# A gate term taken from tables in DRAM by one 48-row matmul, with attention scores, rounding and negations in another order

## The reference

```python
delta_w = jnp.log(w / jnp.swapaxes(w, 1, 2)); delta_h = jnp.log(h / jnp.swapaxes(h, 1, 2))
mul = (100.0 * pos)[..., None] * dim_mat            # pos: delta_x, delta_y, delta_w, delta_h; 2 frequencies
emb = jnp.concatenate([jnp.sin(mul), jnp.cos(mul)], axis=-1)
g = jax.nn.relu(jnp.einsum('bnmd,hd->bhnm', emb, Wg) + bg[None, :, None, None])
a = jnp.einsum('bhqd,bhkd->bhqk', q, k) / jnp.sqrt(jnp.float32(D_K))      # 16 heads of 64
mn = jax.nn.softmax(jnp.log(jnp.clip(g, 1e-06, None)) + a, axis=-1)
out = jnp.einsum('bhqk,bhkd->bqhd', mn, v).reshape(b, nq, H * D_V)
return out @ Wo.T + bo
```

## Time and profile before

| | us |
|---|---|
| median of 3 runs | 1216.48 (1216.2 to 1218.92) |
| the profiled execution: its time | 1219.59 |
| its span, first to last instruction | 1217.7 |
| busy: PE, DVE, ACT, POOL | 988.3, 870.8, 684.9, 723.4 |

### The profile page before, as it was taken

One profiled execution on the slowest core, in us unless ns is written; L12 is line 12 of the kernel. 1 busy time (PEld: TensorE's weight loads), 2 busy tenths in 40 slices (PEclk: granted clock), 3 DMA queues, 4 the chain that ended last, 5 costly groups with the idle time before them and its releaser, 6 DMA issues.

```text
span 1217.7 us, 33080 instructions
## 1 busy us (share of the span) xinstructions
PE 988.3 (81%) x12306; PEld 801.9 (66%) x12306; DVE 870.8 (72%) x1977; ACT 684.9 (56%) x1338; POOL 723.4 (59%) x811
## 2 busy tenths in 40 slices
PE   0548999999999986579878469983899999999995
PEld 0437777776777764445554358862888888888885
DVE  4999998998888876567777789946455555555553
ACT  2446878777887883055526468854444444444442
POOL 2986788885677553024612679947366566566553
PEclk9869999999999997679989689975999999999998
DMA  9165666665766656410001000014442125722141
GB/s 275 54 139 110 120 125 142 138 130 112 132 137 142 124 91 139 163 47 1 1 27 44 1 2 20 19 37 146 134 135 60 30 61 158 238 70 30 26 134 19
DMA packets 48999, 112.99 MB, mean 93 GB/s; under 512 B 6032, under 2 KB 28560, under 8 KB 48512
## 3 DMA queue, kind: packets, MB, share of 16 engines
q0 software_dynamic: 14144, 35.48, 20.2%
q1 hardware_dynamic: 32400, 74.02, 18.3%
q10 hardware_dynamic: 2352, 2.10, 0.5%
HBM read 209.20 MB, written 34.50 MB: 200 GB/s over the span
## 4 chain that ended last, share of the span: by engine, by line
PE 46%; DVE 24%; POOL 11%; issue 9%; ACT 6%; DMA 2%; DVEq 1%; ACTq 0%; POOLq 0%
PE bank L2089 10%; PE bank L2103 7%; POOL PT L534 5%; PE bank L1762 5%; PE bank L1662 2%; PE bank L1719 2%; PE bank L1723 2%; PE bank L1742 2%; DVE nmx L1150 2%; DVE h L1036 2%; PE bank L1701 2%; DVE hf L1267 2%; ACT hm L1603 2%; DVE PT L894 2%; PE bank L1651 2%
## 5 line engine op out<-in xcount | busy, mean ns | idle before, releaser
L1272 DVE TENSOR_TENSOR hm<-hf,hm 128x256 f16<-128x256 f32 x156 | 69.0, 442 | 153.2 <-ACT hm L1603 153.2
L1596 ACT ACTIVATE yg<-bank,bms 128x128 f32<-128x128 f32 x312 | 105.4, 363 | 126.7 <-PE bank L2089 108.2
L2089 PE MATMUL bank<-xT,wm_even 128*128 128x128 f16 x1920 | 117.6, 221 | 14.2 <-DVE hf L1267 13.2
L677 POOL DMA_INDIRECT out_x<-ys,sidx x39 | 62.7, 1607 | 111.8 <-DVE ys L1286 111.8
L2089 PEld LDWEIGHTS bank<-xT,wm_even 128*128 128x128 f16 x1920 | 110.9, 99 | 20.1 <-DVE hf L1267 14.7
L2089 PE MATMUL bank<-xT,wm_odd 128*128 128x128 f16 x1824 | 111.4, 221 | 14.0 <-DVE hf L1267 14.0
L2089 PEld LDWEIGHTS bank<-xT,wm_odd 128*128 128x128 f16 x1824 | 104.9, 99 | 19.3 <-DVE hf L1267 14.1
L1603 ACT ACTIVATE hm<-hf 128x256 f16<-128x256 f32 x156 | 64.7, 415 | 86.2 <-DVE hf L1267 85.4
L534 POOL TENSOR_TENSOR PT<-PT 128x512 f16<-128x512 f32 x64 | 72.2, 1152 | 66.1 <-ACT PT L1394 66.1
L1267 DVE SCALAR_TENSOR_TENSOR hf<-bank,bms,yg 128x128 f32<-128x128 f32 x312 | 94.2, 342 | 8.9 <-ACT yg L1596 8.5
L590 POOL TENSOR_TENSOR h<-h 128x512 f16<-128x512 f32 x32 | 40.6, 1280 | 83.0 <-DVE h L1036 80.9
(11 more groups left out here) (308 smaller groups left out, 2759.1 us busy)
## 6 DMA issues: line engine op xcount, KB each, us to landing
wm_even<-expert_weights SPq DMA_DIRECT2D x60, 1024.0 KB
wm_odd<-expert_weights SPq DMA_DIRECT2D x57, 1024.0 KB
expert_weights<-in_wcat POOLq DMA_DIRECT2D x16, 768.0 KB, 6.9
wsp<-expert_weights SPq DMA_DIRECT2D x16, 768.0 KB, 4.3
wsp<-in_wcat POOLq DMA_DIRECT2D x16, 768.0 KB, 9.7
expert_weights<-wsp SPq DMA_DIRECT2D x16, 768.0 KB, 3.4
expert_tokens<-xs SPq DMA_DIRECT2D x4, 520.0 KB, 5.2
X<-in_x ACTq DMA_DIRECT2D x1, 2048.0 KB, 14.9
```

The costliest lines, as they stand in the source:

```text
L677: nc.gpsimd.indirect_dma_start(out=a["out"], out_offset=bass.IndirectOffsetOnAxis(ap=sidx[:, t:t + 1], axis=0), in_=ys[:, t % 2, :], in_of ...
L1272: v.tensor_tensor(hm16[:, par, 1, c - 1:c + 1, :], hf[:, q % 2, :, :], hm16[:, par, 0, c - 1:c + 1, :], ALU.subtract).then_inc(m_hl, 1)
L1596: s.activation(yg[:, c % 4, :], bank[c % 4][:, 0:MT], ACT.Gelu, bias=bms[:, par, c:c + 1]).then_inc(m_g, 1)
L2089: ins = t.matmul(bank[c % 4][:, w * MT:(w + 1) * MT], wm16[par][:, wp, col:col + P], xT16[:, par, xp * KD + kk, :], start=(n == 0), stop=( ...
```

## The change

1. **Tables over DRAM.** POOL's tables `Lw16` keep one set of eight sequences at a time; DVE splits the other factor once into `R16` (two operations of 128x256 before block 0), and `Rm16`, its mask and its 32 operations are gone. SP stores both in a DRAM tensor in three copies (high, high, low of `Lw16` beside high, low, high of `R16`), six DMAs for each set of eight sequences, and waits until they have landed. For every block it loads three pieces of 16 partitions into `Lst` (48 partitions, two buffers).
2. **One matmul for the separable term** of a gate group: 48 rows of contraction, 128x512, instead of three of 128 rows.
3. **POOL** builds the second set in blocks 0 to 6 (two sequences in block 0, after the first store has landed), no longer in blocks 0 to 7.
4. **PE** computes the second half of the scores after gate group 0, no longer after group 1.
5. **DVE**: rounding and subtraction (`feature_fractions`) come after `residual` in a block.
6. **ACT**: two thirds of the negations come before the first exponential, the last third where all three stood.
7. Two semaphore counters late in the kernel are merged with others; no work changes there.

```diff
+            def store_tables(g):
+                sp.wait_ge(s_pp, 3 + (g + 1) * 5 * NJ)
+                sp.wait_ge(s_whv, 3)
+                for k, (lp, rp) in enumerate(((0, 0), (0, 1), (1, 0))):
+                    sp.dma_start(lst_dram.ap()[g, k, :, 0:GL], Lw16[:, lp, :, :].rearrange("p j c -> p (j c)")).then_inc(s_ts, 16)
+                    sp.dma_start(lst_dram.ap()[g, k, :, GL:], R16[:, g, rp, :]).then_inc(s_ts, 16)
+                sp.wait_ge(s_ts, 96 * g + 96)
+            def load_tables(b):
+                if b > 1:
+                    sp.wait_ge(s_gf, 4 * (b - 1))
+                for k in range(3):
+                    rows = slice(b % 8 * SLOTS, b % 8 * SLOTS + SLOTS)
+                    sp.dma_start(Lst[k * SLOTS:(k + 1) * SLOTS, b % 2, :], lst_dram.ap()[b // 8, k, rows, :]).then_inc(s_tl[b % 2], 16)
             for par in range(2):
                 next_ctx(par, par)
+            store_tables(0)
+            for par in range(2):
+                load_tables(par)
+            for par in range(2):
                 load_half(0, par, True)
             for i in range(1, B // 2 - 1):
                 for par in range(2):
                     next_ctx(i * 2 + par, par)
+                    if i * 2 + par == NJ:
+                        store_tables(1)
+                    load_tables(i * 2 + par)
                     store_half(i - 1, par)
                     load_half(i, par)
...
-                    separable(1, b, b * 5 + (pc.n + 5 * NJ))
+                    if b == 0:
+                        gp.wait_ge(s_ts, 96)
+                        separable(1, 0, pc.n + 5 * NJ)
+                    separable(1, b + 1, (b + 1) * 5 + (pc.n + 5 * NJ))
...
-            def separable(b0, b1):
+            def separable():
                 dv.wait_ge(s_wha, 2)
-                for b in range(b0, b1):
-                    ins = v.tensor_scalar(Rm16[:, b, 0, :], wht[:, 2, b // 8, :], mask[:, b % 8:b % 8 + 1], None, ALU.mult)
...
+                step(v.tensor_copy(R16[:, :, 0, :], wht[:, 2, :, :]))
+                v.tensor_tensor(R16[:, :, 1, :], wht[:, 2, :, :], R16[:, :, 0, :], ALU.subtract).then_inc(s_whv, 1)
...
             def exps(b, par, first):
+                half_negated(b, par, range(NSP - 1))
                 for g in range(4):
                     if g == 2:
-                        half_negated(b, par)
+                        half_negated(b, par, (NSP - 1,))
...
-                for n, (lp, rp) in enumerate(PAIRS):
-                    t.matmul(bk[:, :], Rm16[:, bass.ds(b, 1), rp, :], Lw16[:, grp, lp, 2 * g:2 * g + 2, :], start=(n == 0), stop=(n == 2))
+                t.matmul(bk[:, :], Lst[0:3 * SLOTS, par, GL:], Lst[0:3 * SLOTS, par, g * 512:g * 512 + 512], start=True, stop=True)
```

More of the change, by code:

```diff
@@ L29 @@
 SLOTS = 16
+GL = H * NN * NJ
+GW = GL + N
 WSC = 64.0
@@ L118, in build @@
         Lp = sb("Lp", [P, 2, H, NN], F32, l0)
-        Rm16 = sb("Rm16", [P, B, 2, N], F16, l0)
+        R16 = sb("R16", [P, 2, 2, N], F16, l0)
         We = sb("We", [P, H * NN], F32, l0)
@@ L497, in separable @@
                 gp.wait_ge(s_pp, base + 2)
-                high = Lw16[:, g, 0, bass.ds(j, 1), :].rearrange("p o (h n) -> p (o h) n", h=H)
-                low = Lw16[:, g, 1, bass.ds(j, 1), :].rearrange("p o (h n) -> p (o h) n", h=H)
+                high = Lw16[:, 0, bass.ds(j, 1), :].rearrange("p o (h n) -> p (o h) n", h=H)
+                low = Lw16[:, 1, bass.ds(j, 1), :].rearrange("p o (h n) -> p (o h) n", h=H)
                 nc.gpsimd.tensor_tensor(high, Lp[:, 0, :, :], Lp[:, 1, :, :], ALU.add).then_inc(s_pp, 1)
@@ L972, in iteration @@
                     dv.wait_ge(s_xu, b)
-                else:
-                    separable(0, 2)
+                if has_q:
+                    feature_fractions(b + 1, 1 - par)
                 if not has_q:
@@ L1205, in _ @@
                     ins = top2(i - 3)
-            v4 = Count(m_v)
-            def then(ins):
-                dv.wait_ge(m_v, v4.up(ins))
+            then = step
             idf = xs[:, :, D + 2:D + 4]
@@ L1353, in take_o, with half_negated @@
                     s.activation(OT[:, 4 * r:4 * r + 4, :], bank[6 + r][:, :].rearrange("p (c n) -> p c n", c=4), ACT.Copy).then_inc(s_oc, 1)
-            def half_negated(h, par):
+            def half_negated(h, par, qs):
                 ac.wait_ge(w_ld[par], (h - par) * 8 + 16)
-                for q in range(NSP):
+                for q in qs:
                     c0, c1 = q * HC // NSP, (q + 1) * HC // NSP
@@ L1704, in scores, with gate @@
                                 ins.then_inc(s_st, 1)
-            def gate(b, par, g, first, grp, has_q):
+            def gate(b, par, g, first, has_q):
                 if g == 0:
                     pe.wait_ge(s_flo, b + 1)
-                    if first:
-                        pe.wait_ge(s_whv, 3)
-                        pe.wait_ge(s_pp, 3 + 5 * NJ)
+                    pe.wait_ge(s_tl[par], (b - par) * 24 + 48)
                 n = b + 1 if has_q else b
```

63 lines of the change are left out of this document (26 added, 37 removed).

## The result

| | before | after |
|---|---|---|
| median, us | 1217.38 (1216.2 to 1218.92, 4 runs) | 1200.21 (1199.1 to 1201.81, 4 runs) |
| profiled execution, span | 1219.59, 1217.7 | 1199.1, 1197.2 |
| busy: PE, DVE, ACT, POOL | 988.3, 870.8, 684.9, 723.4 | 966.9, 824.2, 683.6, 722.1 |

The ratio is 0.9859, with a 95% interval of 0.9843 to 0.9875: faster by 1.4%. I had said 1199.5.

A forecast was written before the change was run, and what follows sets the result against it. Bound: a loop through exponentials, ACT, POOL and PE in late blocks, DVE in table blocks. Gains of 8.7 + 1.45 + 2.1 + 1.2 + 3.5 = 17 us from 1219.59, less 3.1, give 1199.5 us; range 1187 to 1212.

The forecast's parts named there:

- Late blocks: Blocks 8 to 13, without a table: earlier second scores and negations bring the probabilities 1.45 us earlier each, 8.7 in all.
- PE's total work is no bound: Late blocks: the loop runs through exponentials, ACT, POOL and PE, so PE's freed 28 us mostly don't count.
- rival D: Late blocks: something else (row maxima, a missed scaling gap) closes the loop; near 24.9 us, total 1212 to 1216; chance 0.07.
- The price of the new gate: PE's gate groups: one table matmul takes 0.22 us, a group 0.88 instead of 1.31, freeing 28 us of PE.
- Blocks 1 to 6: Blocks with POOL's table: DVE is the bound and collides with POOL at the port; 0.2 us each, 1.2 in all.
- Block 7: Block 7 loses its table and becomes a late block; gain 2.1 us.
- Start and block 0: Before and in block 0: the first gate's wait for `Rm16` goes, POOL and port come next; 3.5 us, between 0 and 7.
- Blocks 14 and 15: The last two blocks: block 14 gains 1.45 us like a late block, block 15 is counted as nothing.
- Tables over DRAM: nothing: Stores and loads of the tables stay covered and cost nothing; uncovered, each load would cost 3 to 4 us a block.
- A: Blocks 1 to 6: POOL's and DVE's operations interleave without collisions, start gains 6; 27 us in all, 1189.5; chance 0.12.
- B: Late blocks: a POOL DMA and DVE's distance hold each other up; 0.75 us less gain each, total 1205.5; chance 0.13.
- C: Blocks 0 to 6: POOL keeps the port through a whole table; slower, 1219.5 to 1222 us; chance 0.06.

The follow-up runs named there:

- e1: Changed kernel with the second half of the scores put back behind the first two gate groups on PE; 1206.69 us.
- e2: Changed kernel with all three negations put back together between the two pairs of exponentials on ACT; 1209.43 us.
- e5: Kernel before with only the three order moves (second scores, negations, rounding) and the old tables and gate matmuls; 1212.6 us.
- e4: Changed kernel with second scores, negations and rounding all put back, leaving only the DRAM tables and the single gate matmul; 1208.44 us.
- e9: Changed kernel with the one table matmul of each gate group issued three times into the same place; 1216.8 us.
- e3: Changed kernel with the rounding and subtraction of the next block's features put back before the residual on DVE; 1200.37 us.
- e7: Changed kernel with POOL's early-block tables moved ahead of the low halves of probabilities and features, the last table a block later; 1212.71 us.
- e10: Changed kernel with POOL's second-set tables built in blocks 1 to 7, after waiting for DVE's first product of the block; 1189.82 us.

## Why the prediction was right

The total was right (1199.5 against 1200.21), and the path that the forecast described for the late blocks is the one that the trace shows. But two of its steps gave right numbers for a wrong or incomplete reason.

- **Late blocks.** 1.45 us each predicted, 1.37 measured, by the path I had described: second scores right behind the first pair, two negations under PE's wait, ACT, POOL and `pv` earlier. (The prediction's own times, 327.04 against 325.55, give 1.49.) e1 and e2 show that both moves are needed (0.70 and 1.24 lost).
- **"PE's total work is no bound"** is the step that failed. I read it from PE's pause of 0.62 us ahead of `pv`, and gave the late gain to the orders, with the cheaper gates as time that was free. But PE's busy time in a late block before, 23.74 us, is more than the 23.60 that a late block takes now, so the orders alone could not have given that. e5 shows them worth -0.2 us a block without the cheaper gate, and e4 shows the gate worth 0.15 without the orders; together they give 1.37. Of what e5 lacks against the kernel after (1.56 us), 0.44 is PE's work before `pv` (0.85 in e9) and most of the other 1.1 is the scaling that missed its gap, which rival D had named; had it not, the orders alone would have gained some 0.9 us by my estimate (24.98 - 25.16 + 1.1). The error did not show in the total because the change makes both moves.
- **The price of the new gate** was mis-sized. One matmul was to take 0.22 us and a group 0.88; the group takes 1.08. The table matmul takes 0.32 us up to the next one (313.17 to 313.49), and the six pairwise ones behind it 0.76 instead of 0.65. PE's busy time fell by 21.4 us in all, not 28. Why a matmul of 48 rows costs more than a third of three with 128 is open.
- **Blocks 1 to 6.** 0.2 us each predicted, 0.54 measured for blocks 2 to 6. The collisions came as named (residual 1.34, above 0.9), but the products started 6.97 us after the projection's end where I had counted 7.35. The distance took 2.48, just short of the 2.5 that was to show it. DVE is the bound, as said: e1 and e2 hardly move blocks 2 to 6, and e3 shows that the move of the rounding is their whole gain. Block 1 can't be read by itself. The Trainium skill, page "SBUF — State Buffer", section "Who interferes with whom", calls the port pair an exclusive lock, held for the whole instruction by the one that issues first. The trace agrees: DVE's scaling ends 0.55 us after the POOL operation that was in hand, in both kernels. It does not follow that moving work beside the table gives nothing, since the rounding had taken 4.63 us there before; what is lost depends on which operations meet (2.0 us in the kernel after, 2.7 in e7, nothing in e10).
- **Block 7.** 2.1 predicted, 3.1 measured. It took 26.7 us before, not 25.6: I had charged it the mean of the others, and overlooked that its scaling missed the gap between POOL's splits (1.63 us instead of 0.74, and PE's 1.01 us of waiting for `OT` behind it).
- **Start and block 0.** 3.5 predicted, 4.3 measured, with the low halves at 96.0 where I had said 97. The tables alone give 3.9 of it (e4). PE's half clock in block 0 was in no term.
- **Blocks 14 and 15.** I counted 1.45 and 0. Block 14 gave 2.0 (24.42 against 22.39) and block 15 nothing (31.16 in both).
- **Tables over DRAM: nothing.** No wait for them appears on PE in the kernel after. Only in e7, where the last table came a block later, did they cost: SP's wait for the stores held up the half expert.

The terms of the profiled executions: 4.3 + 0.8 (block 1) + 5 x 0.54 + 3.1 + 6 x 1.37 + 2.0 = 21.1 us up to the last projection, against 17 predicted; the medians give 17.2. The profiled execution of before lay 2.2 us above its median and that of after 1.1 below, so the nearness of the total is partly luck.

**The rivals.** A (no collisions) did not come, as the stretched rows show. e10 is the kernel in which blocks 1 to 6 have none, and its gain against before is 27.6 us, near A's 27; but its start gave 3.4 us and not A's 6, so the nearness is partly luck. B is refuted: the DMA L573 lies at 312.05 in the middle of the distance, and takes 1.21 us beside its 2.14, as both took before, apart from each other. C and D did not come in the kernel after; D's missed gap is in e5 and e9.

## What to carry to other kernels

"This engine has idle time, so less work on it is worth nothing" holds for the loop as it is; when another edit shortens the loop, the idle time is the first thing used up. Compare the engine's busy time with the length that you forecast: here 23.74 us against 23.5. And test two such edits apart and together: here they were worth -0.2, 0.15 and 1.37 us a block.

Where GpSimd and VectorE share a port, don't ask only whether two operations meet but which of the other engine's operations have no need of it. Making the table behind a wait of 0.71 us on GpSimd for the right moment was worth 1.3 us a block against the kernel after; moving VectorE's rounding was worth 0.54.

When a stage is repeated, compare the lengths of its repetitions in two traces, not the totals: in e3, 0.54 us a block was plain while the medians did not show the 3 us.

## What was not expected of the hardware

- **A delay of 0.18 us became one of 1.1.** VectorE's scaling takes 0.74 us when it comes 0.96 us into GpSimd's operation, and 1.68 when it comes 1.14 us in, just behind the start of the next. e5 and e9 show it in every late block, and the kernel before in block 7 alone. By the same rows, the scaling takes 0.73 to 0.75 us in every block from 1 to 13 of the kernel after.
- **Short operations don't slip through.** Beside one table, eight of 0.27 us lost 2.7 us (e7), and in block 0, beside the split of the values and a table, 4.2 us. A single long one can lose as much: the rounding took 4.63 us in e3 and 0.69 where nothing stopped it.
- **Not every end of a GpSimd operation lets VectorE in.** The scaling got in between two of the four splits of the queries. The rounding of e3 came at 184.88, ahead of two splits of the values, and was through only at 189.51, behind those, the context's and the table's first pair. What tells these boundaries apart stays open; no run was made for it.
- **The end of the attention has two clocks.** The same projection took 3.72 or 5.38 us in two kernels that differ in the order of DMAs alone; the stretches that hold it have a granted clock of 0.80 and 1.00 in one and 0.50 and 0.63 in the other. Against it an edit worth 2.2 us in a wait came out as nothing.
